# Score maxima from products over all 128 rows, rows of maxima transposed in the shared PSUM banks, and longer leads for queries and router rows

## The chip, the cores and the metric

The kernel runs on one core of a Trainium2 chip. The metric is the device time of one execution in microseconds (us). The core has five engines, each with its own in-order instruction stream: TensorE (PE, with its weight loads shown as PEld), VectorE (DVE), ScalarE (ACT), GpSimd (POOL) and SyncE (SP, which issues the DMAs here). They meet only through semaphores. PE writes into PSUM, which has eight banks of 128 rows by 512 fp32 columns.

## What is computed

The reference is one transformer layer for 4 sequences of 2048 tokens with width 256: causal attention with 4 heads of 64 and rotary positions, a residual and a layer norm, then a mixture of 32 experts (top 2, capacity limited, with adapters), a residual and a layer norm. The change touches attention and the projections of the router that are woven into it.

```python
q, k = (_rope(q), _rope(k))
energy = jnp.einsum('bhtd,bhld->bhtl', q, k) + mask
attn = jax.nn.softmax(energy, axis=-1)
out = jnp.einsum('bhtl,bhld->bhtd', attn, v)
...
x = _layernorm(x + _L0_attn_ref(x, L0_attn_wq, L0_attn_wk, L0_attn_wv, L0_attn_wo), axis=-1)
...
h = jax.nn.gelu(ri @ r1_w.T + r1_b, approximate=False)
```

## The kernel before

Attention runs over 32 groups. A group `y` is one sequence, one pair of heads and 512 queries; G (0 to 3) says which quarter of the sequence its queries are. The kernel computes the scores twice. First, untransposed, only for the maximum of each query: this is an **entry** `(y, c, i)`, 128 queries `i` against 512 keys `c` for both heads, written to the two banks of `x_ps` ("scores_ps"), read by one DVE reduction into `part_max` (L813). After the last entry of a group DVE reduces `part_max` to `neg_pad` (L818), PE transposes it into rows, and ACT copies those rows into `q_low` (L693, L694), where they serve as a further contraction row that subtracts the maximum. Then the scores are computed transposed, 128 keys by 512 queries and one head at a time: this is a **chunk** (L548 and L550, and L553 on the diagonal), exponentiated by ACT into `probs` (L684), added up by DVE and POOL in turn (L366), and multiplied with the values four chunks at a time (L567). There are 640 chunks and 320 entries.

Numbers are kept to high precision by splitting: `k_st` holds the upper part of a key block in rows 0 to 63 and the lower part in rows 64 to 127; `q_two` holds the upper part of the queries in both halves; `q_low` holds the lower part of the queries, and `k_one` the upper part of the keys with a row of ones for the maxima. In the kernel before, head 0 has its keys in rows 0 to 63 of `k_one` and head 1 in rows 64 to 127, so the two matmuls of an entry (L528) use 64 rows each, and different ones.

The order is written out ahead by `Plan`. It deals the work into 670 slots, one chunk to a slot; in each slot every engine does the `early` steps, then `main` (entries, values, the next chunk's scores two slots ahead), then the `late` steps. `claim` gives a step one of three shared PSUM banks ("misc_a" to "misc_c") at a slot in which no neighbouring slot uses that bank. Steps that matter here:

- `qt` turns a block of queries (L467); `qt_read` splits it (ACT L712, DVE L838). The first entry of a group waits for its queries.
- `wo`, `x1t` and `hidden` are the output projection, the transposition of the normed row and the router's first layer; `ot_read` splits the attention rows ahead of `wo` (ACT L724, DVE L852); `x1t_read` splits the transposed rows (DVE L888, L890) and `hidden` waits for that.
- the rows of maxima are an entry of their own, `(y, None, None)`, in `x_ps` (L514, L515). Every entry waits until the one before it has been read, and the entry behind the rows waits until ACT has read them.

```python
                if e >= 1:
                    kind, count = plan.emptied[e - 1]
                    pe.wait_ge(row_read if kind == "row" else score_read, count)
...
                for hh in range(2):
                    half = slice(hh * HD, (hh + 1) * HD)
                    mm = pe.matmul(x_ps[:, hh, 0:n], q_two[half, ring, hh, cols(i)],
                                   k_one[half, hh, places(f * NT + 4 * c, 4)][:, 0:n], start=True, stop=not diagonal)
```

Before the first slot the kernel projects 12 blocks, sets the ones of `k_one` (DVE L795 to L798), and does the entries of groups 0 and 1. After attention come routing and the experts, which the change does not touch.

## Time and profile before

| what | value |
|---|---|
| median of three runs | 2320.04 us (2317.17 to 2322.69) |
| the profiled execution | 2327.79 us, span 2325.9 us |
| PE busy over the span | 1895.3 us (81%) |
| DVE, POOL, ACT busy | 1533.0, 1330.6, 1214.3 us (66%, 57%, 52%) |
| start, to the first chunk | 0 to 67 us |
| attention, 640 chunks | 67 to 1467 us |
| last output rows, routing | 1467 to 1700 us |
| experts and final norm | 1700 to 2326 us |

The time and the span belong to one execution taken with the profiler; the 1.9 us between them lie outside the first and last instruction. Engines overlap, so busy shares do not add up to the span. A busy PE counts from the first start to the modelled end of matmuls that overlap; what a matmul really costs PE is the distance from its start to the next start. The granted clock is the share of TensorE's 2.4 GHz that it was given; it has two levels, 1.2 and 2.4 GHz, so 0.92 is a mean over time at either.

### The profile page before, as it was taken

The numbers are of one execution on the slowest core, as the hardware profiler recorded it, in microseconds if no ns is written. First come the engines' busy times: TensorE is split into PE (matmuls) and PEld (weight loads), VectorE is DVE, ScalarE is ACT, GpSimd is POOL, SyncE is SP. The second block draws the span as 40 slices with busy tenths as digits, with TensorE's granted clock in tenths as the row PEclk, the third lists the DMA queues.
The fourth block names the chain that finished last, engine by engine and source line by source line (L and its number), as shares of the span: only waits on it lengthen the run. The fifth ranks groups of instructions, "written<-read, shape, count | busy, mean of one in ns | idle before, by whom it ended". The sixth has DMA issues, their size and how long they took to land. (4 is left out here: it accounts for less than half of the span.)

```text
span 2325.9 us, 37201 instructions
## 1 busy us (share of the span) xinstructions
PE 1895.3 (81%) x11170; PEld 1367.0 (59%) x11170; DVE 1533.0 (66%) x3015; ACT 1214.3 (52%) x2965; POOL 1330.6 (57%) x1597
## 2 busy tenths in 40 slices
PE   4699898898998898998898988552176999999990
PEld 3455555555555555555555544451176999999980
DVE  7465676776686785685776685447794655666545
ACT  4245555555455555555555544223264666666655
POOL 2267667677676676676666644210074766667652
PEclk7799999999898998898899989555588999999995
DMA  2000011111011111011111011130003445454428
GB/s 75 5 12 17 17 39 35 40 44 31 16 39 33 42 38 37 15 36 37 37 35 42 10 35 46 41 143 1 0 1 101 135 148 157 156 148 147 147 52 289
DMA packets 100610, 144.07 MB, mean 62 GB/s; under 512 B 17956, under 2 KB 88592, under 8 KB 96364
## 3 DMA queue, kind: packets, MB, share of 16 engines
q1 hardware_dynamic: 84588, 132.04, 16.7%
q0 software_dynamic: 15872, 10.24, 2.7%
q8 instruction: 69, 1.13, 0.2%
q14 instruction: 81, 0.66, 0.1%
HBM read 113.14 MB, written 39.85 MB: 66 GB/s over the span
## 5 line engine op out<-in xcount | busy, mean ns | idle before, releaser
L684 ACT ACTIVATE probs<-scores_t_ps 128x512 f32<-128x512 f32 (+3 forms) x640 | 338.3, 533 | 468.3 <-PE scores_t_ps L550 275.1
L813 DVE TENSOR_REDUCE part_max<-scores_ps 128x2 f32<-128x1024 f32 (+2 forms) x320 | 337.2, 1054 | 142.4 <-PE scores_ps L528 83.7
L366 POOL TENSOR_TENSOR sums<-sums,probs 128x512 f32<-128x512 f32 (+3 forms) x288 | 330.0, 1146 | 33.5 <-ACT probs L684 22.0
L548 PE MATMUL scores_t_ps<-q_two,k_st 128*128 128x512 f32 (+3 forms) x640 | 294.7, 461 | 13.9 <-ACT probs L684 12.7
L567 PE MATMUL out_ps<-probs,v_sb 128*64 128x512 f32 (+3 forms) x1280 | 294.3, 582 | 0.2 <-ACT probs L684 0.2
L1580 PE MATMUL up_ps<-xe_t,w 128*128 128x320 f32 x1920 | 289.7, 311 | 1.7 <-DVE xe_t L1687 1.7
L1580 PEld LDWEIGHTS up_ps<-xe_t,w 128*128 128x128 f32 x1920 | 284.8, 189 | 2.0 <-issue 1.9
L528 PE MATMUL scores_ps<-k_one,q_two 64*128 64x512 f32 (+3 forms) x640 | 158.8, 492 | 107.4 <-DVE part_max L813 55.3
L550 PE MATMUL scores_t_ps<-q_low,k_one 65*128 65x512 f32 (+7 forms) x640 | 243.1, 380 | 0.0
L366 DVE TENSOR_TENSOR sums<-sums,probs 128x512 f32<-128x512 f32 (+3 forms) x288 | 229.4, 796 | 3.2 <-issue 0.6
L548 PEld LDWEIGHTS scores_t_ps<-q_two,k_st 128*128 128x128 f32 x640 | 124.0, 194 | 174.4 <-issue 155.0
L1543 POOL DMA_INDIRECT acc_rows<-out_rows,token x96 | 148.7, 1549 | 127.2 <-ACT out_rows L1670 116.2
L968 POOL TENSOR_TENSOR products<-qk,cos_sin 128x256 f32<-128x256 f32 x116 | 92.4, 797 | 201.4 <-ACT qk L653 177.4
L1701 DVE SCALAR_TENSOR_TENSOR h<-silu,up_ps 128x320 f32<-128x320 f32 x160 | 77.0, 481 | 182.8 <-ACT silu L1657 182.8
L1580 PE MATMUL y_ps<-w,h_parts 128*128 128x256 f32 x1440 | 181.0, 285 | 0.0
L1580 PEld LDWEIGHTS y_ps<-w,h_parts 128*128 128x128 f32 x1440 | 174.4, 191 | 2.2
L528 PEld LDWEIGHTS scores_ps<-k_one,q_two 64*128 64x128 f32 x640 | 63.8, 195 | 184.8 <-DVE part_max L813 89.6
L567 PEld LDWEIGHTS out_ps<-probs,v_sb 128*64 128x64 f32 x1280 | 84.1, 148 | 127.3 <-issue 108.3
L1682 DVE TENSOR_TENSOR w<-w_raw,w 128x768 fp32r<-128x768 f32 x160 | 153.1, 959 | 5.2 <-ACT w L1635 0.9
L1523 POOL DMA_INDIRECT rows<-x_rows,token_in x96 | 129.0, 1344 | 48.0 <-POOL token_in L1520 28.4
L453 PE MATMUL misc_a_ps<-w_qkv,x_t_parts 128*128 128x384 f32 x576 | 145.2, 395 | 1.1 <-DVE q_low L838 1.1
L1635 ACT CAST w<-w_raw 128x768 fp32r<-128x768 f32 x160 | 131.8, 826 | 7.3 <-PEq L1001 7.3
(326 smaller groups left out, 3836.4 us busy)
## 6 DMA issues: line engine op xcount, KB each, us to landing
w_raw<-in_w_expert SPq DMA_DIRECT2D x32, 1536.0 KB, 6.5
x_t<-in_x_t SPq DMA_DIRECT2D x128, 128.0 KB, 2.0
w_raw<-in_w_adapter SPq DMA_DIRECT2D x32, 384.0 KB, 7.1
x_row<-in_x SPq DMA_DIRECT2D x64, 128.0 KB, 2.1
x_rows<-x SPq DMA_DIRECT2D x64, 128.0 KB, 2.0
acc_rows<-x SPq DMA_DIRECT2D x64, 128.0 KB, 2.1
ln_x<-acc_rows SPq DMA_DIRECT2D x16, 512.0 KB, 6.1
out_rows_dram<-ln_y SPq DMA_DIRECT2D x16, 512.0 KB, 5.1
```

Source lines behind the costliest of these rows:

```text
L366: eng.tensor_tensor(side, side, probs[:, g % P_RING, i * P:CH], ALU.add).then_inc(summed[u % 2], 1)
L453: mm = pe.matmul(out, parts_l(a), parts_r(b), start=start and n == 0, stop=stop and n == 2)
L528: mm = pe.matmul(x_ps[:, hh, 0:n], q_two[half, ring, hh, cols(i)], k_one[half, hh, places(f * NT + 4 * c, 4)][:, 0:n], start=True, stop=no ...
L548: pe.matmul(out, k_st[:, hh, places(f * NT + kb)], q_two[:, ring, hh, i * P:CH], start=True, stop=False)
L550: mm = pe.matmul(out, k_one[rows, hh, places(f * NT + kb)], q_low[rows, ring, hh, i * P:CH], start=False, stop=not diagonal)
L567: mm = pe.matmul(o_ps[hh * HD:(hh + 1) * HD, i * P:CH], v_sb[:, place(f * NT + kb), hh, :], probs[:, g % P_RING, i * P:CH], start=kb == 0, ...
L684: act.activation(probs[:, g % P_RING, i * P:CH], s_ps[:, g % 2, i * P:CH], ACT.Exp).then_inc(exp_done, 1)
L813: dve.tensor_reduce(part_max[:, y % 2, :, i, c], x_ps[:, :, 0:n], AX.X, ALU.max).then_inc(score_read, 1)
L1543: pool.indirect_dma_start(out=dram["acc"], out_offset=bass.IndirectOffsetOnAxis(ap=token[0:n, r, t:t + 1], axis=0), in_=out[0:n, r, t, :], ...
L1580: mm = pe.matmul(o, left(a), right(b), start=start and n == 0, stop=stop and n == 2)
L1635: act.copy(columns(w[:, r, 0], p), columns(w_raw[:, r], p)).then_inc(w_upper, 1)
L1682: dve.tensor_tensor(columns(w[:, r, 1], p), columns(w_raw[:, r], p), columns(raw(w[:, r, 0]), p), ALU.subtract).then_inc(w_split, 1)
```

## The change

1. `k_one` keeps both heads' keys in rows 0 to 63 with the ones in row 64, so ACT copies them with one instruction instead of two, and fewer memsets set them up. The two matmuls of an entry now take `k_st` and `q_two` over all 128 rows. The contraction of 64 rows with the adapter for odd heads (`one_rows`) goes, and a chunk's second matmul always has 65 rows.
2. The rows of maxima are no entry any more. They are two steps `row`, one for each head, in two shared banks, two slots behind the wanted slot of the group's last entry (four transpositions of 65 columns each, 64 of them padding). `row_read` on ACT copies one row from each.
3. Leads grow by one slot: an entry stands at the earliest three slots behind its last `qt` (two before), `wo` three behind the step that bounds it (two), `ot_read` two ahead of `wo` (one), `hidden` two behind `x1t` (one). The entries of group 2 may stand two to a slot.
4. The 1/sum rows are spread by 4 matmuls of 64 rows and 128 columns instead of 8 of 4 rows and 64 columns.

```diff
+        for wanted, y, c, i in entries:
+            if y and (c, i) == (self.groups[y][1], 3):
+                for u in (2 * y, 2 * y + 1):
+                    row_at[u] = claim("row", u, max(wanted + 2, 0))
...
-                out_at = claim("wo", m, max(at + 2, out_at + 4))
+                out_at = claim("wo", m, max(at + 3, out_at + 4))
                 turn_at = claim("x1t", m, max(out_at + 7, turn_at + 2))
                 if m % 2:
-                    hidden_at = claim("hidden", m, max(turn_at + 1, hidden_at))
+                    hidden_at = claim("hidden", m, max(turn_at + 2, hidden_at))
...
-            q_from.append(at + 2)
+            q_from.append(at + 3)
...
-            s = max(wanted, at + 1 if at >= 0 else at)
+            at = max(wanted, at + (0 if at < 0 else 0.5 if y == 2 else 1))
...
-            early[at - 1].append(("ot_read", m))
+            early[at - 2].append(("ot_read", m))
...
-                if e >= 1:
-                    kind, count = plan.emptied[e - 1]
-                    pe.wait_ge(row_read if kind == "row" else score_read, count)
...
+                at_least(pe, score_read, e)
...
-                    half = slice(hh * HD, (hh + 1) * HD)
-                    mm = pe.matmul(x_ps[:, hh, 0:n], q_two[half, ring, hh, cols(i)],
-                                   k_one[half, hh, places(f * NT + 4 * c, 4)][:, 0:n], start=True, stop=not diagonal)
+                    mm = pe.matmul(x_ps[:, hh, 0:n], q_two[:, ring, hh, cols(i)],
+                                   k_st[:, hh, places(f * NT + 4 * c, 4)][:, 0:n], start=True, stop=not diagonal)
...
+                elif kind == "row":
+                    out = claim(kind, k, row_read, k + 1)
+                    pe.wait_ge(neg_ready, k // 2 + 1)
+                    for t in range(4):
+                        mm = pe.transpose(out[0:HD + 1, cols(t)], neg_pad[:, t, k % 2, :], ident[:])
+                    mm.then_inc(rows_turned, 1)
...
-                        for hh in range(2):
-                            row = slice(32 * hh, 32 * hh + 4)
-                            mm = pe.matmul(out[hh * HD:(hh + 1) * HD, cols(i)], spread[row, i, :], inverse[row, :],
-                                           start=True, stop=True)
+                        mm = pe.matmul(out[:, cols(i)], spread[0:HD, i].rearrange("p a b -> p (a b)"), inverse[:],
+                                       start=True, stop=True)
...
-                act.copy(k_one[0:HD, 0, places(n)], k_st[0:HD, 0, places(n)])
-                act.copy(k_one[HD:P, 1, places(n)], k_st[0:HD, 1, places(n)]).then_inc(k_again, 1)
+                act.copy(k_one[0:HD, :, places(n)], k_st[0:HD, :, places(n)]).then_inc(k_again, 1)
...
+                elif kind == "row_read":
+                    group, hh = divmod(k, 2)
+                    act.wait_ge(rows_turned, k + 1)
+                    if group >= Q_RING:
+                        act.wait_ge(scores_ready, begin[group - Q_RING + 1])
+                    act.copy(q_low[HD:HD + 1, group % Q_RING, hh, :], bank("row", k)[HD:HD + 1, :]).then_inc(row_read, 1)
...
-            dve.memset(raw(k_one[0:HD, 1, FIRST * P:KEEP * P]), 0.0)
-            dve.drain()
-            dve.memset(raw(k_one[0:1, 1, FIRST * P:KEEP * P]), 1.0)
-            dve.memset(raw(k_one[HD:HD + 1, 0, FIRST * P:KEEP * P]), 1.0).then_inc(ones_set, 1)
+            dve.memset(raw(k_one[HD:HD + 1, :, FIRST * P:KEEP * P]), 1.0).then_inc(ones_set, 1)
```

The first place is on PE at the end of group 15, in the middle of attention. In the kernel before, the rows of group 15 stand in `scores_ps` (L514, L515, four of each, of which the last two are shown) directly ahead of the first entry of group 16 (L528):

```order
L514 MATMUL scores_ps<-ident,neg_pad 65x128
L515 MATMUL scores_ps<-ident,neg_pad 1x128
L528 MATMUL scores_ps<-k_one,q_two 128x128 x2
L532 MATMUL scores_ps<-causal,ident_b 128x128 x2
L548 MATMUL scores_t_ps<-q_two,k_st 128x128
```

In the changed kernel the rows of a group follow chunk work and stand in two shared banks, with key blocks and chunks behind them (here those of group 16):

```order
L536 MATMUL scores_t_ps<-q_two,k_st 128x512
L537 MATMUL scores_t_ps<-q_low,k_one 128x512
L582 MATMUL misc_c_ps<-ident,neg_pad 65x128 x4
L582 MATMUL misc_a_ps<-ident,neg_pad 65x128 x4
L468 MATMUL misc_b_ps<-ident,k_rows 128x128 x2
L536 MATMUL scores_t_ps<-q_two,k_st 128x512
```

The bank that an entry needs is no longer held by rows, so the next entry no longer stands behind ACT's two copies of them.

The second place is on PE ahead of the first entry of group 17: the last turn of its queries is the row with `q_rows` in `misc_b_ps`. Before, one chunk (L548, L550) stands between it and the entry (L528):

```order
L467 MATMUL misc_c_ps<-ident,k_rows 128x128 x2
L467 MATMUL misc_b_ps<-ident,q_rows 128x128 x2
L548 MATMUL scores_t_ps<-q_two,k_st 128x512
L550 MATMUL scores_t_ps<-q_low,k_one 128x512
L528 MATMUL scores_ps<-k_one,q_two 128x512 x2
```

In the changed kernel it stands further ahead of the entry (L516); the second row with `q_rows` belongs to the next group:

```order
L468 MATMUL misc_b_ps<-ident,q_rows 128x128 x2
L554 MATMUL out_ps<-probs,v_sb 64x512 x4
L536 MATMUL scores_t_ps<-q_two,k_st 128x512
L537 MATMUL scores_t_ps<-q_low,k_one 128x512
L468 MATMUL misc_c_ps<-ident,q_rows 128x128 x2
L536 MATMUL scores_t_ps<-q_two,k_st 128x512
L537 MATMUL scores_t_ps<-q_low,k_one 128x512
L468 MATMUL misc_b_ps<-ident,k_rows 128x128 x2
L516 MATMUL scores_ps<-k_st,q_two 128x512 x2
```

Two chunks and a multiplication with the values now stand between the turn and the entry.

The third place is on PE at the last entry of group 17, the one of the four with 512 columns. Before, its rows follow two chunks later:

```order
L528 MATMUL scores_ps<-k_one,q_two 128x512 x2
L532 MATMUL scores_ps<-causal,ident_b 128x128 x2
L548 MATMUL scores_t_ps<-q_two,k_st 128x512
L550 MATMUL scores_t_ps<-q_low,k_one 128x512
L453 MATMUL misc_a_ps<-w_qkv,x_t_parts 128x384 x6
L567 MATMUL out_ps<-probs,v_sb 64x512 x4
L548 MATMUL scores_t_ps<-q_two,k_st 128x512
L550 MATMUL scores_t_ps<-q_low,k_one 128x512
L467 MATMUL misc_c_ps<-ident,q_rows 128x128 x2
L514 MATMUL scores_ps<-ident,neg_pad 65x128
```

In the changed kernel the last entry stands two slots later, and the rows follow one chunk behind it:

```order
L516 MATMUL scores_ps<-k_st,q_two 128x512 x2
L520 MATMUL scores_ps<-causal,ident_b 128x128 x2
L536 MATMUL scores_t_ps<-q_two,k_st 128x512
L537 MATMUL scores_t_ps<-q_low,k_one 128x512
L582 MATMUL misc_b_ps<-ident,neg_pad 65x128 x4
L582 MATMUL misc_a_ps<-ident,neg_pad 65x128 x4
```

The lead of the rows over the last entry went from two slots to none here. The same holds for groups 2, 9, 13, 21, 25 and 29; in the other groups the rows keep their lead of two slots.

## Rows read from the trace of the kernel before

**Rows 1.** The page: span, and the group of DVE's reading of entries.

```profile
span 2325.9 us, 37201 instructions
...
L813 DVE TENSOR_REDUCE part_max<-scores_ps 128x2 f32<-128x1024 f32 (+2 forms) x320 | 337.2, 1054 | 142.4 <-PE scores_ps L528 83.7
```

**Rows 2.** Windows by stage: start:end, length, busy (count) by engine, clock, DMA.

```profile
67.00:1467.00 1400.00, 1245.57 (x6905) 752.01 (x6905) 955.05 (x1866) 730.95 (x2000) 901.22 (x1193) 0.92 0.10 31
...
1700.00:2326.00 626.00, 539.96 (x3808) 523.71 (x3808) 384.89 (x765) 393.56 (x769) 397.44 (x340) 0.93 0.43 138
```

**Rows 3.** Waits of PE from 60 to 1470 us: total, times, longest.

```profile
PE scores_ps L528 <- DVE part_max L813: 54.0, 78, 1.8
PE scores_ps L528 <- DVE q_low L838: 31.9, 14, 3.7
PE scores_ps L528 <- ACT q_low L694: 17.4, 15, 1.3
PE misc_c_ps L453 <- DVE x_ts L890: 13.9, 7, 2.3
...
PE misc_b_ps L453 <- DVE x_ts L890: 6.9, 4, 2.1
PE misc_c_ps L453 <- DVE attn_t L852: 5.0, 11, 0.9
```

**Rows 4.** Timeline of PE around one entry: start, length, instruction.

```profile
107.14 0.40 PE L550 MATMUL scores_t_ps<-q_low,k_one 128*128 128x512 f32 x1
107.47 0.50 PE L528 MATMUL scores_ps<-k_one,q_two 64*128 64x512 f32 x2
107.90 0.50 PE L548 MATMUL scores_t_ps<-q_two,k_st 128*128 128x512 f32 x1
108.24 0.40 PE L550 MATMUL scores_t_ps<-q_low,k_one 65*128 65x512 f32 x1
```

**Rows 5.** Timeline of PE where chunks follow one another.

```profile
702.05 0.40 PE L550 MATMUL scores_t_ps<-q_low,k_one 65*128 65x512 f32 x1
702.29 0.40 PE L548 MATMUL scores_t_ps<-q_two,k_st 128*128 128x512 f32 x1
702.52 0.40 PE L550 MATMUL scores_t_ps<-q_low,k_one 128*128 128x512 f32 x1
702.85 1.07 PE L599 MATMUL misc_c_ps<-sums,pick 128*32 128x128 f32 x16
```

**Rows 6.** Timeline of PE around a diagonal entry, and two 128-column matmuls.

```profile
744.44 0.40 PE L550 MATMUL scores_t_ps<-q_low,k_one 128*128 128x512 f32 x1
744.76 0.44 PE L528 MATMUL scores_ps<-k_one,q_two 64*128 64x384 f32 x2
745.13 0.29 PE L532 MATMUL scores_ps<-causal,ident_b 128*128 128x128 bf16 x2
...
745.78 0.38 PE L467 MATMUL misc_c_ps<-ident,k_rows 128*128 128x128 f32 x2
```

**Rows 7.** Timeline of PE before slot 0: entries back to back, then rows.

```profile
74.13 0.49 PE L528 MATMUL scores_ps<-k_one,q_two 64*128 64x512 f32 x2 [1.32 <-DVE part_max L813]
75.95 0.80 PE L528 MATMUL scores_ps<-k_one,q_two 64*128 64x512 f32 x2 [1.32 <-DVE part_max L813]
...
88.06 0.45 PE L514 MATMUL scores_ps<-ident,neg_pad 128*65 128x128 f32 x1 [1.68 <-DVE neg_pad L818]
```

**Rows 8.** Timeline, ACT and PE, between a group's last query turn and its first entry.

```profile
718.47 0.38 PE L467 MATMUL misc_b_ps<-ident,q_rows 128*128 128x128 f32 x2
...
721.64 0.37 ACT L712 CAST q_two<-misc_b_ps 128x256 fp32r<-128x256 f32 x1
...
722.61 0.50 PE L528 MATMUL scores_ps<-k_one,q_two 64*128 64x512 f32 x2 [3.25 <-DVE q_low L838]
```

**Rows 9.** Windows ahead of and behind that entry; last, ACT's L684 alone in both.

```profile
700.00:723.00 23.00, 19.49 (x125) 12.39 (x123) 14.17 (x34) 15.26 (x41) 17.88 (x24) 1.00 0.16 48
723.00:744.00 21.00, 19.36 (x70) 11.46 (x68) 11.85 (x22) 6.78 (x19) 10.33 (x14) 0.67 0.08 25
...
700.00:723.00 23.00, 6.53 (x11) 1.00 0.16 48
723.00:744.00 21.00, 2.99 (x5) 0.67 0.08 25
```

**Rows 10.** Timeline of the start: setting the ones of `k_one`, then PE.

```profile
46.32 1.34 DVE L795 MEMSET k_one<- 64x1536 f32 x1 [0.38 <-issue]
...
51.16 0.69 PE L467 MATMUL misc_a_ps<-ident,q_rows 128*128 128x128 f32 x2 [6.08 <-DVE k_one L798]
```

More of the change, by code:

```diff
@@ L141, in __init__ @@
             early[spread_at[y] + 1].append(("norm", y))
+        for u, at in row_at.items():
+            assert at <= begin[u // 2] - 3
+            late[at].append(("row", u))
+            early[at + 1].append(("row_read", u))
         turned = {}
@@ L205, in __init__ @@
+            at = max(at, turned.get(f * NT + 4 * c + 3, -100) + 1)
+            s = int(at)
+            assert s <= begin[y] - 5, (y, s, begin[y])
+            self.entries.append((y, c, i))
+            self.last_entry[y] = e
             (self.before if s < 0 else self.score_at[s]).append(e)
-        assert all(self.row_entry[y - 2] < self.last_entry[y] for y in range(2, len(self.groups)))
+            if (c, i) == (G, 3) and y:
+                assert row_at[2 * y - 1] < s <= row_at[2 * y] if y > 1 else s <= row_at[2]
@@ L383, in walk @@
                 score(e)
+            for u in range(2):
+                step("row", u)
+                step("row_read", u)
             for g in range(S_AHEAD):
```

110 lines of the change are left out of this document (33 added, 77 removed).

## Prediction

> **What bounds the kernel now.** The windows by stage come first. Attention takes 1400 of the 2325.9 us; in it PE is busy for 1245.6 us, DVE for 955.1, POOL for 901.2 and ACT for 731.0, and PE's granted clock is 0.92 [rows 1, 2]. The experts take 626 us and the change leaves them alone [rows 2]. So attention decides, PE is its fullest engine, and what can be won there is what PE does, what it waits for, and the clock. The list of PE's waits comes next: in front of entries (L528) it waits 54.0 us for DVE to read the entry before, 31.9 us for queries (`q_low`, 14 times, up to 3.7 us) and 17.4 us for ACT's copies of the rows; in front of the router's first layer 13.9 and 6.9 us for `x_ts`, in front of `wo` 5.0 us for `attn_t` [rows 3]. Third comes the timeline of PE around an entry, read from start to start, since a matmul's modelled length of 0.40 us covers overlap.
>
> **The entry's matmuls.** In the timeline a chunk matmul that follows its like starts 0.235 us after it (702.05, 702.29, 702.52) [rows 5]. Around an entry the distances are 0.33 (107.14 to 107.47), 0.43 (to 107.90) and 0.34 (to 108.24), together 1.10 us [rows 4]. Without the entry the two chunk matmuls among them would take 0.47, so the entry costs PE 0.63 us, although both of its 64-row matmuls run at once. The change makes it two matmuls of 128 rows and 512 columns, like the chunk's: 0.47 us. That is 0.16 us less. The 0.09 us in front of the entry appears as well ahead of a matmul of 32 columns (702.52 to 702.85 is 0.33) [rows 5], so I read it as the price of a change of the array's shape, with another 0.10 on the way back.
>
> On the rule against this change: the Trainium skill, "TensorE: Matmul & The Clock Gate", Part 3, says that matmuls in different row groups run concurrently, and the trace agrees, since the pair takes 0.43 us as one row of the timeline. By that rule alone a pair becomes one pass longer, and the sum would be some 65 us slower on this term instead of 29 us faster. The skill's "TensorEngine Tiling (Array Packing)", Key Properties, says that changing the tiling mode drains the engine; the 0.09 and 0.10 us agree with that.
>
> 192 of the 320 entries are of this kind (32 groups, 4 entries for each of 0 to 3 full key ranges). The other 128 are diagonal, with 128, 256, 384 and 512 columns. At 384 the way in is 0.32 us and the pair 0.37 (744.44, 744.76, 745.13), against two passes of about 0.18; two 128-column matmuls of 128 rows start 0.11 apart (0.38 us together less the 0.27 us of one) [rows 6]. A line through 0.37 and 0.43 gives 0.26 and 0.315 for the small ones; with 0.09 for the way in and against 0.22, 0.24, 0.36 and 0.47 the differences are 0.13, 0.165, 0.10 and 0.05, mean 0.11. In all 192 x 0.16 + 128 x 0.11 = 45 us. An entry that had to wait does not have this gain: its way in lies in the wait. From its start to the second chunk matmul it is 0.43 + 0.34 = 0.77 us now, and with an exposed weight load 0.34 + 0.235 + 0.235 = 0.81 then. Of 107 waits (78 + 14 + 15) [rows 3] I expect the 78 for DVE to stay: 78 x (0.16 + 0.04) = 16 us. **Term: -29 us** (bounds -45 and, if no gain is had, +4).
>
> **DVE's chain.** An entry must be read before the next may be written. Back to back, entries start 1.82 us apart (74.13 to 75.95) [rows 7], of which the reading takes 1.05 in the mean [rows 1]. The second pass makes this chain 0.23 us longer; where PE waits for it, 78 x 0.23 = 18 us at most, and nothing where DVE is late for another reason. I take the middle, **+9 us**.
>
> **Rows in shared banks.** The 17.4 us behind ACT's copies go, since the bank of the entries holds no rows. In the eight groups with G = 3 the first chunk stands close behind its rows and ACT reads them a half slot later than before; the copy takes a few tenths, I put 0.3 us each, 2 us: **-15 us** (0 to -17). In seven groups (2, 9, 13, 17, 21, 25, 29) the rows now stand in the slot of their last entry, and PE waits there for the reading and the reduction. When nothing stood between them this took 1.68 us (88.06) [rows 7]; now one chunk, 0.47 to 0.57 us, lies between, and DVE may be one reading (1.05 us) late. Behind PE's wait the next chunk is queued, so ACT waits too. 7 x 1.5 us: **+10 us** (0 to +17).
>
> **Longer leads.** A slot lasts 1400 / 640 = 2.19 us. The queries of a group were turned at 718.47; ACT came to them at 721.64, and PE stood for 3.25 us at 722.61 [rows 8]. One more slot takes up to 2.19 us off each of the 14 waits; eight of them last 2.5 to 3.7 us and keep about 1 us, the others go: **-22 us** of 31.9 (0 to -32). The waits for `x_ts` are at most 2.3 us, so a slot covers them: **-18 us** of 20.8. For `attn_t` **-4 us** of 5.0. Those steps now stand later in order and nothing is late behind them, since the next `wo` is at least four slots away.
>
> **Start.** DVE's three memsets with their drains hold PE from 46.32 to 51.16 [rows 10], 4.8 us; one over two heads of 1536 columns should take 2 x 1.34 = 2.7: **-2 us**. ACT's saved copy lies beside PE's work and counts nothing, as does the spreading by 4 matmuls (32 times, a change of shape before and after).
>
> **The clock.** Behind the wait at 722.61 the clock is 0.67 for 21 us, in which ACT exponentiates 5 chunks, against 11 in the 23 us at 1.00 before it [rows 9]. At 0.92 over 1400 us, 16% or 224 us of attention run at the lower level, 1.2 GHz. That is 112 us of full-speed time at stake. If the seven waits over 3 us each cost 5 us by what follows them and just over half of that returns: **-20 us** (0 to -60).
>
> **Given back.** The leads and the rows take 15 + 22 + 18 + 4 = 59 us of waits away. PE then comes to DVE and ACT earlier; at 955 of 1400 us DVE has room in the mean but not in the stretches with one entry in each slot. I give a quarter back: **+15 us**.
>
> **Sum:** -29 + 9 - 15 + 10 - 22 - 18 - 4 - 2 - 20 + 15 = -76 us. The profiled execution took 2327.8 us (span 2325.9 and 1.9 around it), so 2252; it lay 8 us above the median of the three runs, and half of that is chance of one execution, so I forecast 2249 us.
>
> **Rivals.** *The clock returns as well.* If the long waits were what took the clock down, 60 us come back instead of 20 and little is given back: 2328 - 76 - 40 - 15 = about 2195. For it: the 0.67 directly behind the wait. Against: the clock is also low in stretches without such a wait.
>
> *The waits move to DVE.* The leads free PE only to stand at the next unread entry; of the 59 us two thirds come back and the clock stays: 2328 - 76 + 20 + 24 = about 2296. For it: 54.0 us for `part_max` is already the largest wait. Against: 445 us in which DVE is idle.
>
> *The packed pair was the cheaper form.* If the 0.09 and 0.10 us belong to an entry's semaphores and not to its shape, they stay, and every pair gains a pass: 192 x 0.235 + 128 x 0.16 = 65 us, with the full 18 us on DVE's chain. Then 65 + 18 + 10 - 59 - 2 + 15 = +47, or about 2370. It decides from where an entry in the middle of chunk work takes over 0.47 + 0.2 us from start to start. The rule on concurrent row groups named above is this case. Against it stands the 0.33 us ahead of the 32-column matmul.
>
> *The leads change nothing.* ACT falls behind by the same slot, and the row steps eat the gain of the pairs: within 0.2% of 2320.
>
> **Chances.** The forecast (2210 to 2280) 0.52, the clock's return 0.18, waits moved to DVE 0.18, no change 0.04, the packed pair 0.08. So faster 0.88, same 0.04, slower 0.08; 0.2% is about what the runs of this kernel can tell from no change. The range 2190 to 2308 takes in the first three but the ends of the second and leaves out the last two. The likeliest case alone reaches from 2210 to 2280.
>
> **What would show it.** In the changed kernel an undisturbed entry followed by a chunk shows distances of about 0.235 throughout; waits of L528's successor for `q_low` fall below 12 us in all, and for ACT's rows to nothing; `x_ts` nearly vanishes; seven waits of 1 to 2.5 us appear ahead of the row transpositions; the clock in attention rises to 0.93 to 0.95. I am wrong if the distances behind an entry keep 0.34, if the wait for `part_max` grows past 80 us, or if the clock falls.

## The result, and the profile after

The changed kernel is slower: 2362.08 us median (2359.60 to 2366.29, four runs) against 2321.16 us for the kernel before (2317.17 to 2322.69, four runs), a ratio of 1.0181 with a 95% interval of 1.0144 to 1.0217. The forecast was 2249 us.

First the page of the changed kernel: the span, and DVE's reading of entries, which answers to [rows 1].

```profile
span 2357.8 us, 36613 instructions
...
L792 DVE TENSOR_REDUCE part_max<-scores_ps 128x2 f32<-128x1024 f32 (+2 forms) x320 | 338.0, 1056 | 130.6 <-PE scores_ps L516 77.1
```

The reading takes as long as it did. The windows by stage (start:end, length, busy and count by engine in the order PE, PEld, DVE, ACT, POOL, then granted clock, DMA share, GB/s) answer to [rows 2]; the first runs from the first chunk's exponential to the last chunk's.

```profile
63.90:1504.40 1440.50, 1252.12 (x6651) 821.85 (x6650) 940.74 (x1865) 698.95 (x1882) 909.88 (x1192) 0.92 0.10 30
1738.00:2357.00 619.00, 540.10 (x3808) 523.92 (x3808) 380.76 (x755) 391.75 (x764) 395.39 (x339) 0.93 0.44 139
```

The same stretch of the kernel before, from its first exponential at 68.1 us to its last at 1466.6 us, reads:

```profile
68.10:1466.60 1398.50, 1244.47 (x6903) 751.43 (x6902) 954.79 (x1865) 730.68 (x1999) 900.82 (x1193) 0.92 0.10 31
```

This stretch, attention, became 42.0 us longer; it begins 4.2 us earlier, and the stages behind it took 5.9 us less of the span. PE's idle time is length less busy time: 154.0 us before, 188.4 us after. The 42 us are 34 us more of idling and 8 us more of PE's busy time, although 252 matmul records went. The clock points the same way: in the clock records of this stretch, time below full level grew from 211.6 to 242.2 us, of which at most half, 15 us, is lost.

PE's waits from 60 to 1510 us (total, times, longest) answer to [rows 3].

```profile
PE scores_ps L516 <- DVE part_max L792: 142.4, 113, 3.7
PE misc_b_ps L582 <- DVE neg_pad L796: 8.6, 7, 1.7
PE misc_b_ps L599 <- DVE k_st L764: 8.2, 8, 1.2
PE misc_b_ps L454 <- POOL x_t_parts L898: 8.1, 3, 2.7
...
PE misc_a_ps L454 <- DVE x_ts L869: 5.2, 8, 0.9
PE scores_ps L516 <- DVE q_low L816: 2.2, 4, 1.0
```

What was to vanish did: the wait for queries fell from 31.9 to 2.2 us, the 17.4 us for ACT's rows are gone, `x_ts` fell from 20.8 to 5.2. But the wait for DVE's reading of the previous entry rose from 54.0 to 142.4 us: 88 us came there, more than the 63 us that those three waits lost. Two more are new, 16.3 us in all: the spreading of the sums (L599) waits for a bank that DVE still reads a key block from, and three projections (L454) wait for POOL's `x_t_parts`.

The timeline of PE around an undisturbed entry answers to [rows 4]: start, length, instruction.

```profile
685.48 0.40 PE L537 MATMUL scores_t_ps<-q_low,k_one 65*128 65x512 f32 x1
685.72 0.64 PE L516 MATMUL scores_ps<-k_st,q_two 128*128 128x512 f32 x2
686.20 0.40 PE L536 MATMUL scores_t_ps<-q_two,k_st 128*128 128x512 f32 x1
686.43 0.39 PE L537 MATMUL scores_t_ps<-q_low,k_one 65*128 65x512 f32 x1
```

The distances are 0.24, 0.48 and 0.23 us: no way in and no way out is left. Such an entry, of the full 512 keys off the diagonal and directly behind a chunk's 512-column matmul, takes a median of 1.10 us before (20 entries that stand undisturbed at the full clock, that is with no wait above 0.25 us) and 0.95 us after (16), counted from the matmul ahead to the second one behind. But few stand so. Most undisturbed entries of this width follow a matmul of 128 columns, a transposition or a mask for example, and there the wide pair itself takes 0.54 to 0.58 us (54 entries). Over all undisturbed entries of this width its median is 0.545 us (89 entries), 0.08 more than two passes, against 0.43 for the packed pair (96). One of these is in the next excerpt, at 746.79: a turn of 128 columns ahead of it, and 0.55 us to the next start at 747.34.

Where the time was lost shows best at a place that comes back every 80 chunks, the start of group 17. An excerpt from the timeline of the changed kernel, DVE, ACT, POOL and PE (idle before and its releaser in brackets):

```profile
743.05 0.96 POOL L927 TENSOR_TENSOR rstd<-mean_var,power 128x1 f32<-128x1 f32 x1 [1.69 <-DVE mean_var L845]
744.08 0.19 POOL L929 TENSOR_TENSOR x_shift<-mean_var,rstd 128x1 f32<-128x1 f32 x1
...
744.31 0.60 ACT L718 ACTIVATE x<-y,x_shift,rstd 128x256 f32<-128x256 f32 x1 [2.89 <-POOL x_shift L929]
...
745.70 0.39 ACT L693 CAST q_two<-misc_b_ps 128x256 fp32r<-128x256 f32 x1
...
746.13 0.42 DVE L816 TENSOR_TENSOR q_low<-misc_b_ps,q_two 64x256 fp32r<-64x256 f32 x1 [2.54 <-ACT q_two L693]
...
746.60 0.44 PE L468 MATMUL misc_b_ps<-ident,k_rows 128*128 128x128 f32 x2 [0.21 <-DVE q_low L816]
...
746.79 0.71 PE L516 MATMUL scores_ps<-k_st,q_two 128*128 128x512 f32 x2
...
747.34 0.40 PE L536 MATMUL scores_t_ps<-q_two,k_st 128*128 128x512 f32 x1
...
747.90 0.42 DVE L816 TENSOR_TENSOR q_low<-misc_c_ps,q_two 64x256 fp32r<-64x256 f32 x1
...
748.81 0.84 DVE L858 SCALAR_TENSOR_TENSOR absolute<-absolute,part 128x256 f32<-128x256 f32 x1
...
749.92 0.43 DVE L764 TENSOR_TENSOR k_st<-misc_b_ps,k_st 64x256 fp32r<-64x256 f32 x1
...
750.38 1.23 DVE L792 TENSOR_REDUCE part_max<-scores_ps 128x2 f32<-128x1024 f32 x1
...
751.66 1.22 PE L516 MATMUL scores_ps<-k_st,q_two 128*128 128x512 f32 x2 [3.69 <-DVE part_max L792]
```

Read it from the top. ACT stands 2.89 us for `x_shift` of the normed row (L718); behind that instruction the queries are queued (L693), and DVE stands 2.54 us for them. The first entry (L516, 746.79) does not wait, as the longer lead promised. But DVE, now late, still has the second query split, the row's statistics (L858 the longest) and a key block ahead of it, and reads the entry only at 750.38, 3.6 us after PE began it. PE waits 3.69 us at the second entry. Before, PE stood one entry earlier at this place, 3.25 us for `q_low` [rows 8]: the wait has moved to the next entry and changed its name. The place is typical of the loss. Over groups 2 to 31 the second entries wait 49.1 us for `part_max` in this kernel, against 10.0 us in the same kernel with short leads (shown below), 39 of the 58 us by which the two differ in this wait; 13 waits for `part_max` last over 2.5 us here and none there.

The clock behind that wait, windows of the changed kernel:

```profile
745.00:752.00 7.00, 3.10 (x15) 2.00 (x14) 5.53 (x13) 4.52 (x14) 6.69 (x9) 0.85 0.06 19
752.00:758.00 6.00, 6.00 (x20) 3.97 (x19) 3.01 (x4) 1.14 (x3) 3.24 (x6) 0.61 0.00 0
```

It answers to the 0.67 of [rows 9]: in the 6 us behind the wait the mean clock is 0.61, most of them at 1.2 GHz.

### The profile page after: what moved, and what is told of

It is laid out like the page before. It is cut to its first block and busy times, and to the rows that moved or that the text cites. A ratio compares the mean times of both kernels' runs of the same rounds, so it can differ in the third digit from the quotient of the medians.

```text
span 2357.8 us, 36613 instructions
## 1 busy us (share of the span) xinstructions
PE 1899.2 (81%) x10914; PEld 1435.6 (61%) x10914; DVE 1516.3 (64%) x3011; ACT 1181.0 (50%) x2837; POOL 1338.8 (57%) x1596
## 3 DMA queue, kind: packets, MB, share of 16 engines
q1 hardware_dynamic: 84588, 132.04, 16.3%
## 5 line engine op out<-in xcount | busy, mean ns | idle before, releaser
L792 DVE TENSOR_REDUCE part_max<-scores_ps 128x2 f32<-128x1024 f32 (+2 forms) x320 | 338.0, 1056 | 130.6 <-PE scores_ps L516 77.1
L516 PE MATMUL scores_ps<-k_st,q_two 128*128 128x512 f32 (+3 forms) x640 | 226.5, 439 | 148.4 <-DVE part_max L792 144.7
L554 PE MATMUL out_ps<-probs,v_sb 128*64 128x512 f32 (+3 forms) x1280 | 288.3, 568 | 0.8 <-ACT probs L674 0.8
L536 PE MATMUL scores_t_ps<-q_two,k_st 128*128 128x512 f32 (+3 forms) x640 | 278.9, 436 | 7.0 <-ACT probs L674 6.2
L537 PE MATMUL scores_t_ps<-q_low,k_one 65*128 65x512 f32 (+3 forms) x640 | 243.9, 381 | 0.0
L516 PEld LDWEIGHTS scores_ps<-k_st,q_two 128*128 128x128 f32 x640 | 113.8, 212 | 198.2 <-DVE part_max L792 181.2
L364 DVE TENSOR_TENSOR sums<-sums,probs 128x512 f32<-128x512 f32 (+3 forms) x288 | 218.4, 758 | 2.9 <-issue 0.8
L898 POOL TENSOR_TENSOR x_t_parts<-x_t,x_t_parts 128x256 fp32r<-128x256 f32 x128 | 101.8, 795 | 82.5 <-ACT x_t_parts L638 82.3
```

What stands on the lines that cost most here:

```text
L364: eng.tensor_tensor(side, side, probs[:, g % P_RING, i * P:CH], ALU.add).then_inc(summed[u % 2], 1)
L516: mm = pe.matmul(x_ps[:, hh, 0:n], q_two[:, ring, hh, cols(i)], k_st[:, hh, places(f * NT + 4 * c, 4)][:, 0:n], start=True, stop=not diagonal)
L536: pe.matmul(out, k_st[:, hh, places(f * NT + kb)], q_two[:, ring, hh, i * P:CH], start=True, stop=False)
L537: mm = pe.matmul(out, k_one[:, hh, places(f * NT + kb)], q_low[:, ring, hh, i * P:CH], start=False, stop=not diagonal)
L554: mm = pe.matmul(o_ps[hh * HD:(hh + 1) * HD, i * P:CH], v_sb[:, place(f * NT + kb), hh, :], probs[:, g % P_RING, i * P:CH], start=kb == 0, ...
L792: dve.tensor_reduce(part_max[:, y % 2, :, i, c], x_ps[:, :, 0:n], AX.X, ALU.max).then_inc(score_read, 1)
```

## Experiments

All ratios are to runs of the kernel before on the same chip, 95% intervals in brackets. The medians of the kernel before lie at 2315 to 2324 us from one set of runs to another, so small differences are read from the ratios. A table at the end of this section puts the waits side by side.

### The wide pair alone

The kernel before, with the two matmuls of an entry over 128 rows. With them PE waits for the lower half of a key block in `k_st` instead of its copy in `k_one`; nothing else changes.

```diff
-                    mm = pe.matmul(x_ps[:, hh, 0:n], q_two[half, ring, hh, cols(i)],
-                                   k_one[half, hh, places(f * NT + 4 * c, 4)][:, 0:n], start=True, stop=not diagonal)
+                    mm = pe.matmul(x_ps[:, hh, 0:n], q_two[:, ring, hh, cols(i)],
+                                   k_st[:, hh, places(f * NT + 4 * c, 4)][:, 0:n], start=True, stop=not diagonal)
```

> The kernel before with one part of the change alone: the two matmuls of an entry take 128 rows. Theory A (the chain of entries decides: PE's product, DVE's reading, next product; a second pass makes each link 0.1 to 0.2 us longer and PE waits it out): 10 to 30 us slower than before, 2330 to 2350 us, with the wait for part_max well above 54 us. Theory B (the pair's gain of some 29 us is real and the loss lies in the longer leads and the moved rows): 15 to 30 us faster, 2290 to 2305 us, with the wait for part_max at 54 to 65 us.

Measured 2315.69 us, 0.9991 [0.9971, 1.0011]: no change, and in the range of neither theory. Its waits:

```profile
PE scores_ps L527 <- DVE part_max L812: 67.2, 88, 1.8
PE scores_ps L527 <- DVE q_low L837: 32.7, 14, 3.7
PE scores_ps L527 <- ACT q_low L693: 17.4, 15, 1.3
```

Here the order of PE is the same as before, so the same entries can be compared. Over the 186 entries of all widths that stand undisturbed at the full clock in both traces, the time from the matmul ahead to the second one behind fell by 0.05 us in the mean; directly behind a chunk's matmul the 17 full-width ones gain 0.17 us in the median, behind shorter matmuls some lose. That would be 17 us if all 320 entries had it, and `part_max` rose by 13 us. So the pair gains little where nothing waits, and about as much is waited away.

### The longer leads alone

The kernel before with all the leads of the change (queries, `wo`, `hidden`, `ot_read`).

```diff
-                out_at = claim("wo", m, max(at + 2, out_at + 4))
+                out_at = claim("wo", m, max(at + 3, out_at + 4))
...
-                    hidden_at = claim("hidden", m, max(turn_at + 1, hidden_at))
+                    hidden_at = claim("hidden", m, max(turn_at + 2, hidden_at))
...
-            q_from.append(at + 2)
+            q_from.append(at + 3)
...
-            early[at - 1].append(("ot_read", m))
+            early[at - 2].append(("ot_read", m))
```

> The kernel before with the longer leads alone (entries three slots behind the last query turn, output projection, its split and the router's first layer a slot further apart); rows stay entries and matmuls of 64 rows. Theory A: the waits for queries and x_ts fall by 30 us or more and 20 to 40 us of that is kept, 2280 to 2300 us. Theory B (DVE and ACT are late for a reason of their own, so PE issues the first entry sooner and then stands just as long in front of the second): same as before or up to 20 us slower, 2318 to 2340 us, with the wait for part_max larger by about what the wait for q_low lost.

Measured 2328.00 us, 1.0036 [1.0013, 1.0059]: slightly slower, though the waits for queries all but went.

```profile
PE scores_ps L528 <- DVE part_max L813: 108.3, 103, 2.3
PE scores_ps L528 <- ACT q_low L694: 13.6, 12, 1.3
PE scores_ps L528 <- DVE q_low L838: 2.7, 5, 1.0
```

Of the waits for `q_low` 29 us went, and `part_max` rose by 54, as theory B had it. So the leads are no gain by themselves either, and the loss of 41 us is not their sum with the pair.

### The changed kernel with the packed pair

The changed kernel with the 64-row matmuls, and the layout of `k_one` and `q_low` with its copies, memsets and one-row transpositions that they need (the diff shows the matmuls alone).

```diff
-                    mm = pe.matmul(x_ps[:, hh, 0:n], q_two[:, ring, hh, cols(i)],
-                                   k_st[:, hh, places(f * NT + 4 * c, 4)][:, 0:n], start=True, stop=not diagonal)
+                    half = slice(hh * HD, (hh + 1) * HD)
+                    mm = pe.matmul(x_ps[:, hh, 0:n], q_two[half, ring, hh, cols(i)],
+                                   k_one[half, hh, places(f * NT + 4 * c, 4)][:, 0:n], start=True, stop=not diagonal)
```

> The changed kernel with the 64-row pair put back (keys of odd heads in rows 64 to 127 again, their ones and maxima in row 0); rows in shared banks and longer leads stay. Theory A: at least 25 us faster than the changed kernel, 2335 us or less. Theory B: as slow as the changed kernel or slower by the pair's lost gain, 2360 to 2390 us.

Measured 2369.51 us, 1.0216 [1.0186, 1.0247], 7 us above the changed kernel, with intervals that overlap. The wide pair did not cause the loss.

### The changed kernel with all leads as before

The reverse of the second experiment's diff.

> The changed kernel with the leads of before (entries two slots behind the last query turn, and so on); 128-row matmuls and rows in shared banks stay. Theory A: the waits for queries and x_ts come back, the time stays at 2355 to 2390 us. Theory B: 20 us or more faster than the changed kernel, 2300 to 2340 us.

Measured 2314.59 us, 0.9972 [0.9949, 0.9995]. The whole loss is gone, and all other parts of the change together bring 0.3%. Which of them makes the leads cost 47 us here, and 9 in the kernel before, no run separates: the pair is ruled out by the run above, but no run has the rows of maxima as entries again.

```profile
PE scores_ps L516 <- DVE part_max L792: 84.0, 89, 2.3
...
PE scores_ps L516 <- DVE q_low L816: 13.8, 11, 1.7
```

### One lead at a time

The changed kernel with only the query lead back (`q_from` at `at + 2`), and with only the three router leads back.

> The changed kernel with only the lead of the queries put back to two slots; the router's steps keep their longer leads. With the short leads all together the time was 0.997 of before, with the long ones 1.018. Theory C (the query lead does the harm: the first entry is issued before DVE can read it, and the next one stands for 3.7 us): 2310 to 2330 us, the longest wait for part_max at most 2.5 us. Theory D (the router's steps do the harm, since output projection, norm and its statistics now fall into the slots in which queries are split and entries stand one to a slot): 2350 us or more, with waits of 3 us and longer left in front of entries.

> The changed kernel with only the router's leads put back (output projection, its split and the router's first layer); the queries keep three slots. Theory C: 2345 us or more, the long waits for part_max stay. Theory D: 2300 to 2325 us, the wait for part_max falls from 142 us below 100.

Measured 2310.96 us, 0.9951 [0.9921, 0.9981], and 2322.39 us, 0.9999 [0.9980, 1.0018]. Each edit alone takes the loss away, so theory C is right in the first run and theory D in the second. Against the kernel with the leads of before (2314.59), the long router leads gain 4 us or nothing, the long query lead loses 8, and both together lose 47. They meet somewhere.

### Half the reading

The changed kernel, with DVE reducing every other key. Half of the scores are left out of the maxima here and in the three runs below that do the same.

```diff
-                dve.tensor_reduce(part_max[:, y % 2, :, i, c], x_ps[:, :, 0:n], AX.X, ALU.max).then_inc(score_read, 1)
+                dve.tensor_reduce(part_max[:, y % 2, :, i, c], x_ps[:, :, 0:n:2], AX.X, ALU.max).then_inc(score_read, 1)
```

> The changed kernel with DVE's reading of an entry cut to every other key, which leaves half of the keys out of the maxima (a softmax may subtract any number near the maximum). DVE's reading falls from 1.05 to about 0.6 us. Theory A (the link of product and reading is what PE waits for): 113 waits fall by 0.4 us each and the time by 40 us or more, to 2320 us or less. Theories C and D (DVE comes late to the entry because it waited for ACT, and ACT for POOL): less than 25 us is gained, 2337 us or more, and waits of 3 us stay.

Measured 2258.13 us, 0.9725 [0.9696, 0.9753], 104 us below the changed kernel. The page's row of the reading:

```profile
L792 DVE TENSOR_REDUCE part_max<-scores_ps 128x2 f32<-128x512 f32 (+2 forms) x320 | 192.8, 603 | 122.0 <-PE scores_ps L516 78.7
```

145 us of DVE's work are gone (338.0 less 192.8), and 104 us of time with it: what DVE has to do between two entries is on the path. That is theory A's time. But the wait for `part_max` fell by 49 us only, to 93.7, and waits of up to 3.2 us stay at the second entries, as theories C and D had it: DVE still comes late there.

### The normed row one slot later

The changed kernel with `x1` (the normed row on ACT), its statistics on DVE and its transposition one slot later.

```diff
-                turn_at = claim("x1t", m, max(out_at + 7, turn_at + 2))
+                turn_at = claim("x1t", m, max(out_at + 8, turn_at + 2))
...
-            early[at + 2].append(("x1", m))
-            late[at + 3].append(("stats", m))
-            late[at + 4].append(("stats2", m))
+            early[at + 3].append(("x1", m))
+            late[at + 4].append(("stats", m))
+            late[at + 5].append(("stats2", m))
```

> The changed kernel with the norm's application on ACT, the statistics behind it and the transposition one slot later, so that ACT comes to it after POOL has the shift. In the changed kernel ACT waits 92 us for POOL's x_shift, and DVE behind it for ACT's q_two. If that wait is where DVE's lateness starts, it falls below 30 us, the wait of PE for part_max below 100 us, and the time to 2330 us or less. If DVE is late for its own load, the time stays at 2350 us or more although ACT's wait is gone.

Measured 2313.19 us, 0.9963 [0.9944, 0.9981], 49 us below the changed kernel with all its leads kept. The time is as expected, the waits are not: ACT's for `x_shift` fell from 91.7 to 35.0 us (below 30 was expected), and PE's for `part_max` from 142.4 to 130.4 (below 100). At the place shown above ACT now takes the queries first and the normed row after them, and DVE stands 0.25 us for the queries instead of 2.54. Yet PE stands there as long as it did. Timeline of that kernel at the start of group 17:

```profile
731.23 0.39 ACT L693 CAST q_two<-misc_b_ps 128x256 fp32r<-128x256 f32 x1
...
731.66 0.42 DVE L816 TENSOR_TENSOR q_low<-misc_b_ps,q_two 64x256 fp32r<-64x256 f32 x1 [0.25 <-ACT q_two L693]
...
732.13 0.60 ACT L718 ACTIVATE x<-y,x_shift,rstd 128x256 f32<-128x256 f32 x1 [0.23 <-POOL x_shift L929]
...
734.42 0.71 PE L516 MATMUL scores_ps<-k_st,q_two 128*128 128x512 f32 x2
...
735.46 0.41 ACT L726 ACTIVATE absolute<-x 128x256 f32<-128x256 f32 x1
735.77 0.37 ACT L653 CAST k_st<-misc_b_ps 128x256 fp32r<-128x256 f32 x1
...
736.17 0.43 DVE L764 TENSOR_TENSOR k_st<-misc_b_ps,k_st 64x256 fp32r<-64x256 f32 x1 [2.51 <-ACT k_st L653]
...
738.05 1.21 DVE L792 TENSOR_REDUCE part_max<-scores_ps 128x2 f32<-128x1024 f32 x1
...
739.32 1.22 PE L516 MATMUL scores_ps<-k_st,q_two 128*128 128x512 f32 x2 [3.72 <-DVE part_max L792]
```

The statistics of the row were moved with it and now stand on ACT ahead of a key block (L726, then L653); DVE stands 2.51 us for that block, reads the entry at 738.05, and PE waits 3.72 us where it waited 3.69. Over groups 2 to 31 the second entries wait 32.1 us, 17 less than in the changed kernel, and 7 waits for `part_max` over 2.5 us are left of 13. So the edit brings 49 us, but at the place walked through it only exchanges what DVE stands for. Of the 44 us by which attention became shorter, 16 are PE's idle time; the rest is PE's busy time, with 57 us less below the full clock (242.2 and 185.5). The edit moves three things, ACT's row step, the statistics and PE's transposition, and no run moves one of them alone.

### Is it one illness, and does the kernel before have it?

Four kernels: the later row step together with the short query lead; half the reading in the kernel before; the later row step in the kernel before; and the changed kernel with all leads as before and the later row step. Their edits are those shown above.

> The changed kernel with the query lead back at two slots and the normed row (with its statistics and its transposition) one slot later. Theory A (one illness: in seven groups of thirty the row step, the last query turn and the next entry meet, and either edit parts them): the two cures do not add, 2300 to 2315 us, within 8 us of the run with the short query lead alone, PE's waits for part_max 100 to 120 us. Theory B (the two edits take away two different delays, worth 51 and 49 us): they add, 2255 to 2275 us, part_max below 90 us. Theory C (a later row step costs on its own and only helped in the setting with long query leads): above 2318 us.

Measured 2281.51 us, 0.9819 [0.9782, 0.9856], with 111.4 us for `part_max`. Neither theory: the two edits do not add in full (2262 us), but the later row step gains 29 us where the query lead is short already. The meeting of row step and query turn is not all that it cures.

> The kernel before with DVE reducing every other key of an entry, so that half of the scores are left out of the maxima; nothing else changes. Reading an entry of 512 keys takes some 0.5 us less, over 320 entries about 105 us of DVE's work. Theory A (DVE's chain from entry to entry is what PE runs into in both kernels): most of the 54 us for part_max go and queries are split earlier, 60 to 90 us less, 2235 to 2260 us, as in the changed kernel with the same edit (104 us less). Theory B (the reading limits only where the longer leads have put PE against it): not more than part of the 54 us, 20 to 35 us less, 2287 to 2302 us.

Measured 2248.48 us, 0.9685 [0.9636, 0.9735], 75 us below the kernel before. DVE's chain is what PE runs into in the kernel before as well; `part_max` fell from 54.0 to 21.8 us, the waits for queries stayed:

```profile
PE scores_ps L528 <- DVE q_low L838: 31.2, 14, 3.7
PE scores_ps L528 <- DVE part_max L813: 21.8, 42, 1.1
PE scores_ps L528 <- ACT q_low L694: 17.4, 15, 1.3
```

> The kernel before with the normed row, its statistics and its transposition one slot later. In its plan too the row step and the last query turn stand in one slot ahead of groups 9, 13, 17, 21, 25 and 29. Theory A (ACT, waiting for the row's shift, is late for the queries there): PE's wait for q_low falls from 32 us below 22, and the time to 2295 to 2312 us. Theory B (the meeting costs only where an entry stands one per slot right behind it, as in the changed kernel): q_low stays above 28 us, 2316 to 2326 us.

Measured 2289.45 us, 0.9859 [0.9823, 0.9896], more than expected. ACT's wait for the shift fell from 54.7 to 18.5 us, PE's for queries to 21.7, but `part_max` rose to 69.7; PE, less held at the queries, may stand at the reading sooner.

> The changed kernel with all leads as before and the normed row one slot later. Against the same kernel without the later row (2314.6 us): theory A (the row step holds ACT ahead of the queries whatever the leads are): 8 to 20 us less, 2295 to 2307 us, with the waits for q_low at or below 10 us. Theory B (with short leads the row step is not what makes queries or entries late): 2310 to 2319 us.

Measured 2278.94 us, 0.9811 [0.9775, 0.9847], 36 us below the same kernel without the later step, far beyond the 8 to 20 us expected. This version beats both kernels. But it did not do so as theory A says: PE's wait for `q_low` did not fall below 10 us but rose from 13.8 to 14.6, and `part_max` from 84.0 to 89.1. PE's idle time in attention fell by 16 us elsewhere, most of it in front of the router and the projections (for `x_ts` from 26.3 to 15.7 us) and behind ACT's exponentials (6.6 to 0.9). Nor was there a meeting to undo: in the order written by `Plan`, the row step shares its slot with the last query turn of a group in 12 groups of the changed kernel, and of the same kernel with the short query lead, but in none with the short router leads. Why the later row step helps there stays open.

### Why the query lead costs, and how far the row step can go

Counted in the traces, the entries with only one chunk between them and the one before are 96 in the kernel before, 123 in the changed kernel with short query leads and 138 with the long one. `q_from` moves no turn, only entries. It moves the first entry of 22 groups, but the last one of only seven, so in the others a later start is made up for by entries in neighbouring slots. Half the reading, now with the short query lead and with all short leads, asks whether that is what costs.

> The changed kernel with the query lead back at two slots, and DVE reducing every other key, so that half of the scores are left out of the maxima. With the long query lead and half the reading it took 2258 us; with whole reading the query lead alone made 2362 against 2311 us. Theory A (the longer query lead costs because entries then follow one another in neighbouring slots more often, and DVE's reading can't keep up): with half the reading the lead costs little, so this run lies at 2240 to 2258 us. Theory B (the lead costs by where it puts the entries against row step and sums, whatever the reading takes): the difference stays, 2205 to 2225 us.

Measured 2246.15 us, 0.9700 [0.9655, 0.9745].

> The changed kernel with all leads as before and DVE reducing every other key, so that half of the scores are left out of the maxima. With whole reading the leads together made 2362 against 2315 us. Theory A (as above): with half the reading the long leads are no loss any more, even a gain of the waits for queries and router rows that they take away, so this run lies at 2250 to 2275 us, within 10 us of the same kernel with long leads (2258 us) or above it. Theory B: some 47 us below that, 2205 to 2220 us.

Measured 2242.69 us, 0.9677 [0.9633, 0.9720]. The first run lies in theory A's range, the second in neither, 7 us below A's. With half the reading the long query lead costs 12 us instead of 51, and all long leads together 15 instead of 47 (6 and 11 us by the ratios); the intervals overlap. So most of what the leads cost goes through the time DVE needs to read; a small rest may be real.

> The changed kernel with all leads as before and the normed row, its statistics and its transposition two slots later instead of one (2279 us with one). ACT still waits 42 us for the row's shift there. Theory A (what ACT waits for the shift delays queries and entries): half of those 42 us go and the time falls by 5 to 15 us, 2264 to 2274 us. Theory B (one slot took the waits that matter): 2275 to 2283 us.

Measured 2281.23 us, 0.9850 [0.9805, 0.9894]: no more gain, as theory B had it, though ACT's wait for the shift in attention went from 30.4 to 6.8 us. `part_max` and `q_low` fell by 11.5 us more, but PE's waits for `attn_t` rose from 4.6 to 14.2 us and those in front of the sums from 0.5 to 9.7. So the second slot moved waits; that the first took all that mattered is not shown.

Waits in attention in us (`part_max` and `q_low` are PE's, `x_shift` is ACT's), and entries with one chunk between them and the one before:

| kernel | median us | `part_max` | `q_low` | `x_shift` | close entries |
|---|---|---|---|---|---|
| before | 2321.2 | 54.0 | 31.9 | 54.7 | 96 |
| before, wide pair | 2315.7 | 67.2 | 32.7 | 57.0 | 96 |
| before, long leads | 2328.0 | 108.3 | 2.7 | 77.9 | 124 |
| changed, short leads | 2314.6 | 84.0 | 13.8 | 64.4 | 123 |
| changed, router leads long | 2311.0 | 115.0 | 14.2 | 93.9 | 123 |
| changed, query lead long | 2322.4 | 98.7 | 1.0 | 60.6 | 138 |
| changed | 2362.1 | 142.4 | 2.2 | 91.7 | 138 |
| before, row step later | 2289.5 | 69.7 | 21.7 | 18.5 | 97 |
| changed, row step later | 2313.2 | 130.4 | 1.0 | 35.0 | 138 |
| changed, query lead short, row step later | 2281.5 | 111.4 | 18.3 | 36.5 | 123 |
| changed, short leads, row step later | 2278.9 | 89.1 | 14.6 | 30.4 | 117 |
| changed, short leads, row step two later | 2281.2 | 80.8 | 11.4 | 6.8 | 114 |

## Why the prediction was wrong

**The entry's matmuls** (-29). The mechanism was right, the size was not. Behind a chunk's matmul the way in and the way out went as read, and the rival of the packed pair, for which the Trainium skill's rule on concurrent row groups ("TensorE: Matmul & The Clock Gate", Part 3) spoke, fell: packed again, the kernel was no faster. The skill's "TensorEngine Tiling (Array Packing)", Key Properties, on the drain at a change of mode agrees with the 0.10 us that went behind an entry. What failed is that every undisturbed entry was priced as the one of [rows 4], between two chunk matmuls of 512 columns. There the pair takes 0.47 us and the gain is the 0.16 forecast. But of the 96 undisturbed entries of 512 keys off the diagonal in the trace of before only 20 stand so; behind a matmul of 128 columns the wide pair takes 0.54 to 0.58 us. With the pair alone the mean gain of an undisturbed entry is 0.05 us instead of the 0.14 (45 us over 320) that was counted on, and the time did not change.

**DVE's chain** (+9). `part_max` rose by 13 us with the wide pair alone: about right.

**Rows in shared banks** (-15 and +10). The 17.4 us went, and the seven waits of the same-slot groups cost 8.6 us, with one more of 1.2. The sizes are right, but a side effect was left out: rows that claim shared banks push other steps. The order has the last query turn of group 17 at slot 296 before and 298 after, that of group 9 at 135 and 138, so entries start later there and stand closer; this is argued, not shown, to be how the close entries came to 123 even with the leads as before, for no run moves the rows alone. The spreading's 8.2 us for a bank with a key block, which the kernel before lacks, belongs here too.

**Longer leads** (-22, -18, -4). They did take away the waits that they aimed at. The step that failed is the sentence behind them, "nothing is late behind them", together with **given back** (+15). The reason given looked at the next `wo` alone, not at the queries, key blocks and readings that share ACT's and DVE's queues. A quarter of 59 us was put back; measured, the wait for `part_max` alone rose by 88 us. The prediction knew that DVE's room is a mean, and still let three quarters of the gain stand. At the start of group 17 DVE's room was no use: it spent 2.54 us of it standing for ACT, with the steps that stood ahead of the reading still to do. The rival "the waits move to DVE" had the right mechanism, but its 2296 us let two thirds return and held the clock. Two things go with the loss. The longer query lead moves only entries and packs them closer (123 to 138), and with the longer router leads ACT's waits for `x_shift` rise (64 to 94 us), ahead of queries and key blocks for which DVE waits before it reads. Neither costs much alone: 94 us of such waits with the short query lead go with 2311 us, 138 close entries with the short router leads with 2322. Shown is that each lead alone costs little and both together some 47 us, that the later row step takes 49 us off, and that with half the reading most of the leads' cost is gone. That DVE is late because ACT stands for POOL is seen at one place; the later row step took that wait away and left PE's wait there as it was, so as the cause of the 47 us it is argued, not shown. Why the leads cost more in the changed kernel than in the one before stays open as well.

**The clock** (-20). It went the other way: the time below full level grew by 31 us, at most 15 us lost. Against the changed kernel with short leads it is 242 to 164 us, up to 39 us; attention is 55 us longer there, 27 us of it PE's idling and 28 its busy time. Over all executions the mean granted clock is 0.876 in the changed kernel (4), 0.882 in the kernel before (25) and 0.887 with short leads (10). But time at the lower level is not all lost: the wide pair alone has 0.890, and no less time for it. That the clock was 0.61 directly behind the wait shown is in the trace; why it comes down there stays open. The kernel before with long leads has no wait of 2.5 us in attention and still 207 us at the lower level, so the length of single waits does not settle it. No experiment held the clock alone.

**Start** (-2). The first chunk came 4.2 us earlier, but the seventeenth 9.7 us later (its exponential at 123.5 and 133.2 us): the entries of group 2 stand two to a slot there, and PE waits for `part_max` up to 2.01 us (at 101.0 us). With short leads it is 132.0 us, so the leads are not the reason. This part was not tried by itself.

Two of the things that the prediction named as its own refutation came true: a wait for `part_max` above 80 us, and a clock that falls. One slip of the sum changes nothing: 2252 us less half of 8 is 2248, not 2249.

## What to carry to other kernels

A wait that is taken away is a gain only as far as the next thing in line has room *at that place*; read the queue of the engine behind the wait, instruction by instruction, before the mean idle time of that engine is called room. A longer lead with an unchanged due time packs the work behind it, so count what stands closer. And look for the engine that waits with others' work queued behind it: here the row step, whose first instruction on ACT stood for POOL, brought 29 to 49 us in four kernels when it was moved one slot later. Then look again at the place that was to be cured, since the time can fall for another reason.

## What the runs showed of the hardware

Going from 64-row matmuls in two row groups to 128-row ones took away the 0.10 us behind an entry. Two 512-column passes with different weights took 0.47 us behind another 512-column matmul, and 0.55 us behind a transposition of 128 columns (746.79 in the excerpt on group 17); the packed pair took 0.43 us in both places. DVE's maximum over two PSUM banks went by elements read, also with a stride of two: 1.21 us for 128x1024, 0.69 for 128x512 side by side, and 0.68 for 128x512 at a stride of two. POOL's two instructions on 128x1 columns, `rstd` and `x_shift`, took 0.96 and 0.19 us at the place shown (0.75 and 0.20 in the mean of 64), the first alone longer than ACT's exponential of a chunk (0.53 us in the mean).
